# Two-layer latent transformer on one core: layer norms taken one token tile at a time, four landing places for the last head's values, and a reordered lead-in to the expert stage

## The chip, the core and the metric

The kernel runs on one core of a Trainium2 chip. The core has a matrix engine (PE, with its weight loads listed as PEld), a vector engine (DVE), an activation engine (ACT), GpSimd (POOL) and a queue engine (SP) that issues most transfers; sixteen DMA engines move the data. The five engines run their own instruction streams and meet at semaphores: one engine adds to a semaphore when an instruction is done, another waits for a value. The metric is the time of one execution in microseconds; lower is better.

## The reference

Six residual steps on a state `x` of 256 tokens by 512 features, each behind a layer norm without weights. The context has 4096 rows of 512.

```
x = x + cross_attention(norm(x), ctx)        # 16 heads of 128
x = x + attention_fp8(norm(x))               # 16 heads of 32, q, k, v rounded to e4m3 with one scale each
x = x + relu_ffn(norm(x)) + gate * expert    # 8 gate logits, 2 best
x = x + memory_attention(norm(x), ctx)       # scores against ctx, the 54 best of 4096 kept
x = x + attention(norm(x))                   # 16 heads of 32, with biases
x = x + moe(norm(x))                         # 64 experts, 8 per token, at most 64 tokens each
```

`norm(x)` is `(x - mean) / sqrt(var + 1e-5)` over the 512 features of a token.

## The kernel before

Everything is float32; where a product needs less time, an operand is split into a high and a low part of type fp32r and three products replace one. The 256 tokens are two tiles of 128 (`TT = 2`, `x[:, 0]` and `x[:, 1]`), the 512 features four blocks (`DT = 4`). The order of the work on each engine is written out by hand: one function for each engine and stage (`tensor_attention`, `vector_memory` and so on), called one after the other at the end of the program.

**The norm.** `vector_norm` takes the statistics of both tiles (L116, L119), adds the epsilon (L121), waits for GpSimd's power of -1/2 (L133) and writes the normed tiles `xn` (L126). `tensor_norm` fills PE's time with products of the identity (`stay_awake`, L138), then transposes the tiles (L146), and `scalar_norm` copies them to `xT` (L153), features on the partitions. Each stage's products wait for both tiles.

**Cross attention.** The 16 heads run one after the other; a head's 4096 keys are eight chunks of 512 (`NCH = 8`). The values of all heads are computed once and kept in DRAM (`v_dram`). For each chunk GpSimd loads them back (L867) into `v_back`, and from head 12 on (`LATE`) in turn into `v_back` and `v_late`. In the last head no keys are left to compute, so a chunk is only: DVE subtracts the maximum (`shift`, L694), ACT raises (L538) and rounds to `e_hi` (L547), DVE forms `e_lo` (L714), and PE multiplies by the values (`weigh`, L405, 12 products) and by ones for the sums (L410, 8 products). `load_v(n + 1)` waits until `weigh` has finished with the chunk that held its place. SP meanwhile loads the weights of the next stage (L950), one megabyte each for queries, keys and values, as `e_lo` of every second chunk is done.

**Attention, twice** (`k = 0` with quantisation, `k = 1` without). PE computes the eight feature blocks of queries and keys for both tiles (256 columns each), then the values of tile 0 and tile 1. For `k = 0` DVE needs the largest magnitude of all queries, GpSimd spreads it over the partitions, ACT and DVE round to e4m3, and then the same for the keys; only then do the scores start (L974).

**Feed-forward.** Products with `w_up`, then for each tile the gate, the expert and `w_down`.

**Memory attention.** Queries for both tiles, 16 blocks of scores (12 products each), a search for the 54 best on DVE, transposes of the weights (L1400), 16 blocks of products with the context (`weigh_chunk`, L1410), and for each tile a transpose (L1417) and the output product.

**Experts (MoE).** Router products and top 8 give `mask`, and ranks by products with triangular ones give `slot`, the place of a token in its expert. `make_sel` turns slots into 0/1 matrices `sel`; `gather` multiplies the tokens (`xn_hi`, `xn_lo`) by them. The slots also go transposed as `slotT` to DRAM and back as `slot_all`, spread over the partitions (L1663, L1666), for `make_selT` (L1839), which `spread_out` needs. The 64 experts are 32 pairs in groups of four; a turn of the loop is `up` (L1712), a `gather` of the next group, `down` (L1732, L1733), `spread_out` (L1741) and `turn` (L1723); once per group `find_gates` multiplies `sel` by the gate weights, 8 products. Weights of a pair come 2.3 MB at a time into a ring of seven.

A float32 product shows as two records in the trace, an fp32r product and a transpose as one.

## Time and profile before

| | |
|---|---|
| time of three runs | 1778.22, 1778.88, 1780.69 us, median 1778.88 |
| profiled execution | 1774.9 us, its span 1772.9 us |
| busy: PE / DVE / ACT / POOL | 1704.4 / 1088.1 / 693.3 / 96.4 us |
| granted PE clock over the span | 0.991 of full speed |
| instructions | 23791 |

The span runs from the first to the last instruction; around it the profiled execution has 2.0 us more. The busy time of PE includes the products of the identity, which compute nothing. A granted clock of 1 is 2.4 GHz; the other level is 1.2 GHz.

### The profile page before, as it was taken

Reading aid. Unit: us, or ns where it says so; the run is one execution under the profiler, and the core shown is the slowest. Engines: PE = TensorE matmul, PEld = TensorE weight load, DVE = VectorE, ACT = ScalarE, POOL = GpSimd, SP = SyncE. Lnnn points to the kernel's source line nnn. Section 1 sums busy time; section 2 is a strip of 40 time slices with the busy share of each in tenths; the row PEclk is TensorE's granted clock in tenths of the full one; section 3 lists DMA queues with packets and bytes.
Section 4 is the critical chain, followed back from the end, with each engine's and each line's share of the span. In section 5 each row is a group of like instructions: output and inputs, shape, how many; then the busy total and the mean of one; then the engine's idle time right before and its main releaser. Section 6 shows DMA issues by size and latency. Waiting matters only on the chain.

```text
span 1772.9 us, 23791 instructions
## 1 busy us (share of the span) xinstructions
PE 1704.4 (96%) x9438; PEld 1343.0 (76%) x9438; DVE 1088.1 (61%) x1738; ACT 693.3 (39%) x937; POOL 96.4 (5%) x177
## 2 busy tenths in 40 slices
PE   8998999999999999999999999978899999899998
PEld 7887888887888888788888788876577466554544
DVE  4446777777677777777777788965538315333333
ACT  4334444445444444444444555542213212212121
POOL 0000000000000000000000010010000000000000
PEclk9999999999999999999999999999999999999999
DMA  6755544445455454454454522252104181488880
GB/s 220 207 166 155 131 131 131 126 131 149 121 132 143 121 137 123 140 143 119 131 136 125 132 96 88 86 192 94 49 1 190 48 356 81 102 307 324 306 323 33
DMA packets 114733, 262.55 MB, mean 148 GB/s; under 512 B 6656, under 2 KB 76480, under 8 KB 108480
## 3 DMA queue, kind: packets, MB, share of 16 engines
q1 hardware_dynamic: 96192, 193.93, 35.5%
q0 software_dynamic: 18432, 67.12, 12.6%
q8 instruction: 75, 1.23, 0.3%
q14 instruction: 34, 0.28, 0.1%
HBM read 193.35 MB, written 67.67 MB: 147 GB/s over the span
## 4 chain that ended last, share of the span: by engine, by line
PE 64%; issue 24%; DVE 5%; DMA 3%; POOL 2%; ACT 1%; SPq 0%; POOLq 0%; DVEq 0%; ACTq 0%
PE bank L41 16%; PE bank L392 14%; PE bank L364 10%; PE bank L405 5%; PE bank L1712 5%; PE bank L1410 3%; PE bank L1733 2%; PE bank L1732 2%; PE bank L138 2%; PE bank L1741 2%; POOL v_back L867 1%; DMA v_dram<-v_out 1%; PE bank L1019 1%; DMA slot_all<-slots_dram 1%; PE bank L430 1%
## 5 line engine op out<-in xcount | busy, mean ns | idle before, releaser
L714 DVE TENSOR_TENSOR e_lo<-S,e_hi 128x1024 fp32r<-128x1024 f32 x128 | 156.6, 1223 | 94.1 <-ACT e_hi L547 93.8
L364 PE MATMUL bank<-cT_hi,wk_hi 128*128 128x512 f32 x512 | 205.6, 402 | 0.0
L392 PE MATMUL bank<-wv_hi,cT_hi 128*128 128x512 f32 x512 | 199.9, 390 | 3.5 <-DVE wv_lo L651 3.5
L364 PE MATMUL bank<-cT_hi,wk_lo 128*128 128x512 f32 x512 | 200.5, 392 | 0.0
L392 PE MATMUL bank<-wv_hi,cT_lo 128*128 128x512 f32 x512 | 199.4, 390 | 0.0
L364 PE MATMUL bank<-cT_lo,wk_hi 128*128 128x512 f32 x512 | 199.2, 389 | 0.0
L392 PE MATMUL bank<-wv_lo,cT_hi 128*128 128x512 f32 x512 | 199.2, 389 | 0.0
L538 ACT ACTIVATE S<-S 128x1024 f32<-128x1024 f32 x128 | 135.6, 1059 | 157.9 <-DVE S L694 157.8
L547 ACT CAST e_hi<-S 128x1024 fp32r<-128x1024 f32 x128 | 134.7, 1052 | 152.3 <-PE bank L405 142.7
L707 DVE TENSOR_TENSOR esum<-esum,S 128x512 f32<-128x512 f32 x210 | 145.1, 691 | 71.9 <-ACT S L538 68.3
L405 PE MATMUL bank<-e_hi,v_back 128*128 128x256 f32 x896 | 170.6, 288 | 12.2 <-DMA v_back<-v_dram 4.3
L682 DVE TENSOR_TENSOR mx<-mx,S 128x512 f32<-128x512 f32 x224 | 154.3, 689 | 15.1 <-ACT S L532 11.2
L41 PE MATMUL bank<-q_hi,k_hi 128*128 128x256 f32 x512 | 145.5, 284 | 15.6 <-ACT S L532 8.0
L694 DVE TENSOR_TENSOR S<-S,mrow 128x1024 f32<-128x1024 f32 x128 | 155.1, 1216 | 1.3 <-POOL mrow L873 1.3
L405 PEld LDWEIGHTS bank<-e_hi,v_back 128*128 128x128 f32 x896 | 141.8, 193 | 18.1 <-issue 11.6
L41 PE MATMUL bank<-q_lo,k_hi 128*128 128x256 f32 x512 | 145.6, 284 | 0.0
L41 PE MATMUL bank<-q_hi,k_lo 128*128 128x256 f32 x512 | 145.5, 284 | 0.0
L518 ACT CAST k_hi<-bank 128x512 fp32r<-128x512 f32 x128 | 75.1, 587 | 166.6 <-PE bank L364 166.6
L532 ACT COPY S<-bank 128x1024 f32<-128x1024 f32 x128 | 128.8, 1006 | 10.2 <-PE bank L41 10.2
L405 PE MATMUL bank<-e_lo,v_back 128*128 128x256 f32 x448 | 127.3, 284 | 0.0
L41 PEld LDWEIGHTS bank<-q_hi,k_hi 128*128 128x128 f32 x512 | 98.1, 192 | 23.9 <-DVE k_lo L669 10.1
L669 DVE TENSOR_TENSOR k_lo<-bank,k_hi 128x512 fp32r<-128x512 f32 x128 | 87.9, 687 | 45.3 <-ACT k_hi L518 45.3
(265 smaller groups left out, 2899.8 us busy)
## 6 DMA issues: line engine op xcount, KB each, us to landing
w<-in_w_moe SPq DMA_DIRECT2D x32, 2304.0 KB, 8.5
v_dram<-v_out SPq DMA_DIRECT2D x112, 512.0 KB, 4.6
v_back<-v_dram POOLq DMA_DIRECT2D x112, 512.0 KB, 5.0
v_dram<-v_back SPq DMA_DIRECT2D x16, 512.0 KB, 3.9
v_late<-v_dram POOLq DMA_DIRECT2D x16, 512.0 KB, 3.5
ctx_nat<-in_ctx SPq DMA_DIRECT2D x8, 1024.0 KB, 4.6
ctx_raw<-in_ctxT SPq DMA_DIRECT2D x7, 1024.0 KB, 8.0
l_w_qkv<-in_l_wqkv SPq DMA_DIRECT2D x6, 1024.0 KB, 6.0
```

Source lines behind the costliest of these rows:

```text
L41: last = e.matmul(dst, lhs, rhs, start=(n == 0), stop=(n == len(terms) - 1))
L364: t = e.matmul(banks[b][:], l, r, start=(c == 0 and m == 0), stop=(c == DT - 1 and m == 2))
L392: t = e.matmul(banks[b][:], l, r, start=(c == 0 and m == 0), stop=(c == DT - 1 and m == 2))
L405: t = e.matmul(banks[O_BANK][:, 0:T], v[:, i, l, :], r[:, i, :], start=(j == 0 and i == 0 and m == 0), stop=(j == NCH - 1 and i == CT - 1 ...
L532: e.copy(S[:, j * CT:(j + 1) * CT, :].rearrange("p a t -> p (a t)"), twin[:]).then_inc(s_stored, 1)
L538: e.activation(Sj, Sj, ACT.Exp).then_inc(raised, 1)
L547: e.copy(e_place(n)[0][:], S[:, j * CT:(j + 1) * CT, :]).then_inc(e_rounded, 1)
L682: own.done(e.tensor_tensor(mx[:], mx[:], two, ALU.max))
L694: e.tensor_tensor(Sj, Sj, mrow[:].unsqueeze(1).to_broadcast([P, CT, T]), ALU.subtract).then_inc(shifted, 1)
L707: e.tensor_tensor(esum[:], esum[:], two, ALU.add).then_inc(e_summed, 1)
L714: e.tensor_tensor(lo[:], Sj, hi[:].bitcast(F32), ALU.subtract).then_inc(e_split, 1)
L1712: t = e.matmul(banks[UP_BANKS[p % 2]][rows, 0:2 * FF], xg[:, g % 2, c, at:at + P // 2], ring[p % N_RING][:, s * UPW + c * 2 * FF:s * UPW + ...
```

## The change

**The norm by tiles.** `norm_stats`, `norm_apply`, `norm_turn` and `norm_move` each take one tile, and GpSimd raises one column at a time. Each stage is then laid out anew around them:

- in attention 0, tile 0's values are multiplied before tile 1 is transposed; queries and keys come behind that, for both tiles;
- in the feed-forward, gate and expert of tile 0 stand before tile 1's transpose, and tile 0's norm is taken while PE still projects tile 1's attention output;
- in memory attention, tile 0's queries stand before tile 1's transpose, and tile 1's queries between the second and the third block of scores; the seven small operations of `find_coefficient` stand between tile 1's statistics and its norm;
- in attention 1, the transpose of tile 0 and its queries, keys and values stand in the end of the memory stage, around tile 1's output product.

**Values in four places.** For the last head's eight chunks the values land in turn in `v_back`, `v_late`, `v_tail0` and `v_tail1`; the two new places lie on buffers that the last keys have left. The loads of chunks 1, 2 and 3 are issued together, each later one when the chunk four before it has been weighed.

**The lead-in to the experts.** The router and its logits go by tiles. `xn_hi` and `xn_lo` are formed early. The slots are transposed and moved out before the first `gather`, and `slot_all` comes in two parts, first the four pairs of the first group, then the other 28, for which only `make_selT(4)` waits. The gate weights are split into two fp32r parts, so that `find_gates` has 8 fp32r products of 4 columns for 8 float32 products of 2 columns.

```diff
+        def norm_stats(e, n, i):
+
+            own.done(e.bn_stats(stats[:, i, :], x[:, i, :]))
             own.wait(e)
-            for i in range(TT):
-                own.done(e.bn_aggr(meanvar[:, i, :], stats[:, i, :]))
+            own.done(e.bn_aggr(meanvar[:, i, :], stats[:, i, :]))
             own.wait(e)
-            e.tensor_scalar(vareps[:], meanvar[:, :, 1], EPS, None, ALU.add).then_inc(ln_var, 1)
...
+            e.tensor_scalar(vareps[:, i:i + 1], meanvar[:, i, 1:2], EPS, None, ALU.add).then_inc(ln_var, 1)
+
+        def norm_apply(e, n, i, xn):
+            e.wait_ge(ln_rstd, TT * n + i + 1)
+            e.tensor_scalar(xn[:, i, :], x[:, i, :], meanvar[:, i, 0:1], rstd[:, i:i + 1], ALU.subtract, ALU.mult).then_inc(ln_xn, 1)
...
-            e.wait_ge(ln_var, n + 1)
-            e.tensor_tensor(rstd[:], vareps[:], half[:], ALU.pow).then_inc(ln_rstd, 1)
+            for i in range(TT):
+                e.wait_ge(ln_var, TT * n + i + 1)
+                e.tensor_tensor(rstd[:, i:i + 1], vareps[:, i:i + 1], half[:, i:i + 1], ALU.pow).then_inc(ln_rstd, 1)
...
+        def norm_turn(e, n, i, xn, bank):
+
+            e.wait_ge(ln_xn, TT * n + i + 1)
+            for c in range(DT):
+                t = e.transpose(bank[:, c * P:(c + 1) * P], xn[:, i, c * P:(c + 1) * P], ident[:])
+            t.then_inc(ln_turned, 1)
...
+            b = late % 2 if n < TAIL else (n - TAIL) % 4
+            turns = late // 2 if n < TAIL else (TAIL - LATE * NCH) // 2 * (b < 2) + (n - TAIL) // 4
+            return (v_back, v_late, v_tail0, v_tail1)[b], v_in[b], 16 * (turns + 1 + (LATE * NCH if b == 0 else 0))
...
+            xn1 = att_mem[0][5]
+            for i in range(TT):
+                add_tile(h, i)
+                e.wait_ge(x_added, TT * h + i + 1)
+                norm_stats(e, 1, i)
+            for i in range(TT):
+                norm_apply(e, 1, i, xn1)
...
+                elif n - TAIL in (2, 3):
+                    e.wait_ge(scored, NH)
+                    e.wait_ge(k_projected, NH)
+                elif n > TAIL + 1:
+                    e.wait_ge(weighed, n - 3)
...
+                    elif n < TAIL:
                         load_v(n + 1)
+                    elif n == TAIL:
+                        for ahead in (1, 2, 3):
+                            load_v(n + ahead)
+                    elif n + 3 < NH:
+                        load_v(n + 3)
...
+        def project_qk(e, k, features, lo, hi):
+
+            w = att_mem[k][0]
+            for f in features:
+                if f % 4 == 0:
+                    e.wait_ge(att_w_in[f // 4], ATT_W[k])
+                t = matmuls(e, banks[f // 2][:, f % 2 * T + lo:f % 2 * T + hi],
+                            [(w[:, f // 4, c, f % 4 * P:(f % 4 + 1) * P], xT[:, c, lo:hi]) for c in range(DT)])
+                if f % 2 and hi == T:
+                    t.then_inc(qk_projected, 1)
+
+        def project_values(e, k, i):
+            w = att_mem[k][0]
+            e.wait_ge(att_w_in[2], ATT_W[k])
+            e.wait_ge(ln_xT, TT * (1 if k == 0 else 4) + i + 1)
+            matmuls(e, banks[4 + i][:], [(xT[:, c, i * P:(i + 1) * P], w[:, 2, c, :]) for c in range(DT)]).then_inc(av_projected, 1)
...
+            if k == 0:
+                stay_awake(e, banks[0], 12)
+                norm_turn(e, 1, 0, xn, banks[0])
+                stay_awake(e, banks[3], 2)
+                project_values(e, k, 0)
+                norm_turn(e, 1, 1, xn, banks[1])
+                e.wait_ge(ln_xT, TT * 2)
+                project_qk(e, k, range(8), 0, T)
+                project_values(e, k, 1)
+            else:
+                norm_turn(e, 4, 1, xn, av_bank(1))
+                stay_awake(e, av_bank(0), 2)
+                e.wait_ge(ln_xT, TT * 5)
+                project_qk(e, k, range(8), P, T)
+                project_values(e, k, 1)
...
             for i in range(TT):
+                own.done(e.tensor_tensor(x[:, i, :], x[:, i, :], b_out[:], ALU.add))
+            own.wait(e)
+            n_norm, xn_next = ((2, xn3), (5, xn6))[k]
+            for i in range(TT):
                 n = TT * k + i
...
                 e.tensor_tensor(x[:, i, :], banks[2 + i][:], x[:, i, :], ALU.add).then_inc(att_added, 1)
+                e.wait_ge(att_added, n + 1)
+                norm_stats(e, n_norm, i)
+                norm_apply(e, n_norm, i, xn_next)
...
+            norm_turn(e, 2, 0, xn3, banks[0])
+            stay_awake(e, banks[4], 2)
+            e.wait_ge(ln_xT, TT * 2 + 1)
+            gate(0)
+            expert(0)
+            norm_turn(e, 2, 1, xn3, banks[1])
+            stay_awake(e, banks[4], 2)
             e.wait_ge(ln_xT, TT * 3)
...
+            gate(1)
+            e.wait_ge(up_moved, DT // 2)
+            down(0)
+            expert(1)
+            down(1)
...
+            weights(0)
+            add_expert(0)
+            weights(1)
+            add_shared(0)
+            norm_apply(e, 3, 0, xn4)
+            add_expert(1)
+            add_shared(1)
+            find_coefficient(e)
+            norm_apply(e, 3, 1, xn4)
...
+                    if n == 2:
+                        project_q4(1)
+                    if n == NCH:
+                        e.wait_ge(q4_split, TT)
...
+            def project_q4(i):
+                tok = slice(i * P, (i + 1) * P)
+                e.wait_ge(*landed["w_q4"])
+                e.wait_ge(ln_xT, TT * 3 + i + 1)
+                for f in range(DT):
+                    t = matmuls(e, q4_bank(f)[:, tok], [(w_q4[:, c, f * P:(f + 1) * P], xT[:, c, tok]) for c in range(DT)])
+                t.then_inc(q4_projected, 1)
+
+            norm_turn(e, 3, 0, xn4, banks[0])
+            stay_awake(e, twin, 2)
+            project_q4(0)
+            norm_turn(e, 3, 1, xn4, banks[1])
+            stay_awake(e, banks[score4_bank(0)], 4)
+            e.wait_ge(q4_split, 1)
             score_tile(0)
             score_tile(1)
             for s in range(TT * NCH + 1):
                 if s < TT * NCH:
                     turn(*divmod(s, NCH))
+                if s == TT * NCH:
+                    norm_turn(e, 4, 0, att_mem[1][5], av_bank(0))
                 if s:
                     weigh_chunk(*divmod(s - 1, NCH))
                 if s == NCH + 2:
                     turn_av(0)
                 if s == NCH + 4:
                     project_out(0)
+            e.wait_ge(ln_xT, TT * 4 + 1)
+            e.wait_ge(p_moved, TT * NCH)
+            project_qk(e, 1, range(4), 0, P)
             turn_av(1)
+            project_qk(e, 1, range(4, 8), 0, P)
             project_out(1)
+            project_values(e, 1, 0)
...
-                e.dma_start(slot_all[rows], by_half[s].unsqueeze(0).to_broadcast([P // 2, PAIRS, T])).then_inc(slots_in, 16)
+                e.dma_start(slot_all[rows, 0:FIRST], by_half[s, 0:FIRST].unsqueeze(0).to_broadcast([P // 2, FIRST, T])).then_inc(slots_in, 16)
+            e.wait_ge(slots_in, 32)
+            for s, rows in enumerate(halves):
+                e.dma_start(slot_all[rows, FIRST:], by_half[s, FIRST:].unsqueeze(0).to_broadcast([P // 2, PAIRS - FIRST, T])).then_inc(slots_in, 16)
...
-                    two = slice(EPP * (GROUP * g + n), EPP * (GROUP * g + n + 1))
-                    t = matmuls(e, TURN_B[:, 2 * P + 2 * n:2 * P + 2 * n + 2],
-                                [(sel[:, g % 2, i, pair].bitcast(F32), gate_w[:, i, two]) for i in range(TT)])
+                    t = matmuls(e, TURN_B[:, 2 * P + 4 * n:2 * P + 4 * n + 4],
+                                [(sel[:, g % 2, i, pair], gate_parts[:, i, GROUP * g + n, :, :]) for i in range(TT)])
...
             for i in range(TT):
-                matmuls(e, banks[2][:, i * E:(i + 1) * E],
+                stay_awake(e, banks[i], 2 + 8 * i)
+                norm_turn(e, 5, i, xn6, banks[i])
+                stay_awake(e, banks[4], 2)
+                e.wait_ge(ln_xT, TT * 5 + i + 1)
+                matmuls(e, banks[2 + i][:, 0:E],
                         [(xT[:, c, i * P:(i + 1) * P], w_router[:, c, :]) for c in range(DT)]).then_inc(routed, 1)
...
-            for c in range(DT):
-                gather(0, c)
             e.wait_ge(slot_made, 1)
             for i in range(TT):
                 t = e.transpose(TURN_B[0:E, i * P:(i + 1) * P], slot[:, i, :], ident[:])
             t.then_inc(slot_turned, 1)
+            for c in range(DT):
+                gather(0, c)
...
             for i in range(TT):
+                e.wait_ge(logits_moved, i + 1)
                 own.done(e.max(route(i, 8, 16), logit[:, i, :]))
+                if i == 0:
+                    e.wait_ge(xn_rounded, 1)
+                    e.tensor_tensor(xn_lo[:], xn6[:], xn_hi[:].bitcast(F32), ALU.subtract).then_inc(xn_split, 1)
...
-            e.wait_ge(xn_rounded, 1)
-            e.tensor_tensor(xn_lo[:], xn6[:], xn_hi[:].bitcast(F32), ALU.subtract).then_inc(xn_split, 1)
+            e.wait_ge(slot_turned, 1)
+            e.tensor_copy(slotT[:], TURN_B[0:E, 0:T]).then_inc(slot_moved, 1)
...
+                high, low_part = gate_parts[:, i, :, 0, :], gate_parts[:, i, :, 1, :]
+                gates = gate_w[:, i, :].rearrange("p (n s) -> p n s", s=EPP)
+                own.done(e.tensor_scalar(high, gates, route(i, 2), None, ALU.mult))
+                own.wait(e)
+                e.scalar_tensor_tensor(low_part, gates, route(i, 2), high.bitcast(F32), ALU.mult, ALU.subtract).then_inc(route_gate, 1)
```

The core of the diff is shown; left out are declarations, renamings and the same steps on ACT.

**Three places in the order of instructions.** The first is GpSimd's stream at the last head: `v_...<-v_dram` is one load of a chunk's values (L867, in the new kernel L887), `mrow<-mxr` the maximum of the last head over the partitions, for which the head's first `shift` waits. Before:

```order
L867 DMA v_late<-v_dram 128x1024
L873 ISA mrow<-mxr 128x256
L867 DMA v_back<-v_dram 128x1024
L867 DMA v_late<-v_dram 128x1024
L867 DMA v_back<-v_dram 128x1024
L867 DMA v_late<-v_dram 128x1024
```

Now:

```order
L887 DMA v_late<-v_dram 128x1024
L887 DMA v_tail0<-v_dram 128x1024
L887 DMA v_tail1<-v_dram 128x1024
L893 ISA mrow<-mxr 128x256
L887 DMA v_back<-v_dram 128x1024
L887 DMA v_late<-v_dram 128x1024
L887 DMA v_tail0<-v_dram 128x1024
L887 DMA v_tail1<-v_dram 128x1024
```

Two loads moved ahead of the maximum, and four are left behind it instead of six.

The second is PE's stream between the last head and the first scores of attention 0 (`l0_xn` is the normed state, `l0_w_qkv` the weights; 256 wide are queries and keys of both tiles, 512 wide the values of one tile). Before:

```order
L138 MATMUL bank0<-ident 128x128 x20
L146 MATMUL bank0<-ident,l0_xn 128x128 x4
L146 MATMUL bank1<-ident,l0_xn 128x128 x4
L138 MATMUL bank3<-ident 128x128 x2
L41 MATMUL bank0<-xT,l0_w_qkv 128x256 x8
L41 MATMUL bank1<-xT,l0_w_qkv 128x256 x8
L41 MATMUL bank2<-xT,l0_w_qkv 128x256 x8
L41 MATMUL bank3<-xT,l0_w_qkv 128x256 x8
L41 MATMUL bank4<-l0_w_qkv,xT 128x512 x4
L41 MATMUL bank5<-l0_w_qkv,xT 128x512 x4
```

Now:

```order
L135 MATMUL bank0<-ident 128x128 x12
L141 MATMUL bank0<-ident,l0_xn 128x128 x4
L135 MATMUL bank3<-ident 128x128 x2
L41 MATMUL bank4<-l0_w_qkv,xT 128x512 x4
L141 MATMUL bank1<-ident,l0_xn 128x128 x4
L41 MATMUL bank0<-xT,l0_w_qkv 128x256 x8
L41 MATMUL bank1<-xT,l0_w_qkv 128x256 x8
L41 MATMUL bank2<-xT,l0_w_qkv 128x256 x8
L41 MATMUL bank3<-xT,l0_w_qkv 128x256 x8
L41 MATMUL bank5<-l0_w_qkv,xT 128x512 x4
```

The values of tile 0 and tile 1's transpose moved ahead of all queries and keys.

The third is PE's stream from the last block of products with the context (`ctx_nat`) to the values of attention 1 (`av` is the memory attention's result, `w_o4` its output weights). Before:

```order
L1410 MATMUL bank5<-ctx_nat,pT 128x512 x8
L1417 MATMUL bank67<-ident,av 128x128 x4
L41 MATMUL bank3<-w_o4,xT 128x512 x4
L138 MATMUL bank0<-ident 128x128 x14
L146 MATMUL bank0<-ident,l1_xn 128x128 x4
L146 MATMUL bank1<-ident,l1_xn 128x128 x4
L138 MATMUL bank3<-ident 128x128 x2
L41 MATMUL bank0<-xT,l1_w_qkv 128x256 x8
```

Now:

```order
L141 MATMUL bank67<-ident,l1_xn 128x128 x4
L1495 MATMUL bank5<-ctx_nat,pT 128x512 x4
L41 MATMUL bank0<-xT,l1_w_qkv 128x128 x8
L41 MATMUL bank1<-xT,l1_w_qkv 128x128 x8
L1502 MATMUL bank67<-ident,av 128x128 x4
L41 MATMUL bank2<-xT,l1_w_qkv 128x128 x8
L41 MATMUL bank3<-xT,l1_w_qkv 128x128 x8
L41 MATMUL bank5<-w_o4,xT 128x512 x4
L41 MATMUL bank4<-l1_w_qkv,xT 128x512 x4
L141 MATMUL bank67<-ident,l1_xn 128x128 x4
L135 MATMUL bank67<-ident 128x128 x2
L41 MATMUL bank0<-xT,l1_w_qkv 128x128 x8
```

The 14 products of the identity are gone, and tile 0's queries, keys and values stand on both sides of tile 1's output product.

## Rows read from the trace of the kernel before

**Rows 1.** Three stretches: us, busy of PE, PEld, DVE, ACT, POOL, granted clock, DMA share, GB/s
```profile
1180.60:1184.50 3.90, 3.82 (x20) 3.69 (x20) 1.43 (x2) 0.00 (x0) 0.00 (x0) 0.62 0.93 342
...
1529.70:1534.10 4.40, 4.40 (x18) 1.59 (x18) 1.61 (x4) 0.00 (x0) 0.00 (x0) 0.62 0.78 142
...
1545.20:1740.00 194.80, 194.80 (x943) 98.12 (x943) 63.83 (x182) 38.97 (x78) 0.00 (x0) 1.00 0.79 300
```
**Rows 2.** Timeline of PE, last head: start, us, instruction [idle before <- releaser]
```profile
1172.99 0.48 PE L405 MATMUL bank<-e_hi,v_late 128*128 128x256 f32 x2 [1.16 <-DVE e_lo L714]
...
1175.90 0.50 PE L405 MATMUL bank<-e_hi,v_back 128*128 128x256 f32 x2 [0.28 <-DMA v_back<-v_dram]
...
1180.68 0.50 PE L405 MATMUL bank<-e_hi,v_late 128*128 128x256 f32 x2 [2.13 <-DMA v_late<-v_dram]
...
1193.90 0.50 PE L405 MATMUL bank<-e_hi,v_back 128*128 128x256 f32 x2 [2.70 <-DMA v_back<-v_dram]
...
1200.16 0.28 PE L410 MATMUL bank<-e_lo,ones_r 128*128 128x256 f32 x1
```
**Rows 3.** Timeline of ACT and DVE, last head, chunk 4
```profile
1178.59 1.04 ACT L547 CAST e_hi<-S 128x1024 fp32r<-128x1024 f32 x1 [0.92 <-PE bank L410]
...
1179.66 1.22 DVE L714 TENSOR_TENSOR e_lo<-S,e_hi 128x1024 fp32r<-128x1024 f32 x1 [0.56 <-ACT e_hi L547]
```
**Rows 4.** Timeline of POOL before the last head
```profile
1161.52 0.53 POOL L867 DMA_DIRECT2D v_late<-v_dram  x1 [2.32 <-PE bank L405]
1163.11 1.06 POOL L873 PARTITION_ALL_REDUCE mrow<-mxr  x1 [1.07 <-DVE mxr L687]
```
**Rows 5.** Timelines of DVE and PE, norm and products of attention 0
```profile
1207.81 1.39 DVE L126 TENSOR_SCALAR l_xn<-x,meanvar,rstd 128x512 f32<-128x512 f32 x2 [0.87 <-POOL rstd L133]
1218.45 1.22 DVE L1138 TENSOR_REDUCE l_sc<-l_qkT 128x1 f32<-128x1024 f32 x1 [9.25 <-ACT l_qkT L1085]
...
1208.80 1.11 PE L146 MATMUL bank<-ident,l_xn 128*128 128x128 f32 x8 [0.73 <-DVE l_xn L126]
...
1210.62 14.08 PE L41 MATMUL bank<-xT,l_w_qkv 128*128 128x256 f32 x64 [0.26 <-ACT xT L153]
1224.54 7.03 PE L41 MATMUL bank<-l_w_qkv,xT 128*128 128x512 f32 x16
```
**Rows 6.** Timeline of PE, from attention 0's output product to the feed-forward
```profile
1277.14 3.29 PE L138 MATMUL bank<-ident 128*128 128x128 f32 x28
...
1283.13 7.17 PE L41 MATMUL bank<-xT,w_up 128*128 128x256 f32 x32 [0.25 <-ACT xT L153]
```
**Rows 7.** Timeline of PE, from the feed-forward to the memory scores
```profile
1305.66 3.29 PE L138 MATMUL bank<-ident 128*128 128x128 f32 x28
...
1320.17 0.50 PE L41 MATMUL bank<-cT_hi,qT_hi 128*128 128x512 f32 x1 [0.29 <-DVE qT_lo L1582]
```
**Rows 8.** Timeline of PE, from the memory stage to attention 1's scores
```profile
1423.42 7.03 PE L1410 MATMUL bank<-ctx_nat,pT 128*128 128x512 f32 x16
...
1442.34 14.08 PE L41 MATMUL bank<-xT,l_w_qkv 128*128 128x256 f32 x64 [0.26 <-ACT xT L153]
...
1463.22 1.14 PE L974 MATMUL bank<-l_qkT 32*128 32x256 f32 x12
```
**Rows 9.** Timelines of DVE and PE, start of the expert stage
```profile
1521.78 1.22 DVE L1889 TENSOR_TENSOR xn_lo<-xn,xn_hi 128x1024 fp32r<-128x1024 f32 x1
...
1527.32 0.42 DVE L1899 CAST slotT<-bank 64x256 bf16<-64x256 f32 x1 [3.06 <-PE bank L1761]
...
1543.60 0.35 DVE L1839 TENSOR_SCALAR selT<-slot_all,slot_col 128x256 fp32r<-128x256 bf16 x1 [7.10 <-DMA slot_all<-slots_dram]
...
1527.88 1.92 PE L41 MATMUL bank<-gate_w,sel 128*128 128x2 f32 x16 [0.60 <-DVE slotT L1899]
1529.73 4.43 PE L1712 MATMUL bank<-w,xg 128*64 128x384 f32 x16
...
1544.78 0.44 PE L1723 MATMUL bank<-ident,h 128*128 128x128 f32 x2 [2.81 <-DVE h L1855]
```

232 lines of the change are left out of this document (104 added, 128 removed).

## The prediction

> **What bounds the kernel now.** I read the chain of waits first: it runs through PE's products almost everywhere, with DVE, ACT and DMA links only in the seams between stages. The stretches by window confirm it: in the expert loop PE is busy all 194.8 us at full granted clock [rows 1], so there only fewer PE records help. Then I read each engine's timeline around every norm and at the end of cross attention, for what PE waits for there. The reader should see three things. In the last head PE waits for values from DRAM, up to 2.70 us before a chunk [rows 2], and then runs some products at a lower clock, 0.62 on average in one stretch [rows 1]. At each norm PE fills 3.29 us with identity products and then still waits, because nothing starts until both tiles are normed, turned and copied [rows 5 to 8]. At the start of the expert stage a transfer, `slot_all`, holds DVE for 7.10 us and through it PE for 2.81 us [rows 9].
>
> **The last head.** Chunk 1 starts at 1172.99 and chunk 2 could have started at 1175.90 - 0.28 = 1175.62, so a chunk takes 2.63 us when its values are there [rows 2]. Does another engine hold a chunk longer? `e_hi` of chunk 4 starts when chunk 2 has left its buffer, and ACT's 1.04 and DVE's 1.22 us after it end at 1180.88 [rows 3], 2.3 us after that start; chunk 3 is weighed meanwhile, which is the longer. So seven chunks follow 1172.99 at 2.63: end at 1191.4, against 1200.44 now [rows 2]: **-9.0**. The four loads now go out some three chunks (7.9 us) before their use instead of one. But the four loads (0.5 MB each) and three blocks of attention weights (1 MB each) must move 5.2 MB before the last chunk starts at 1188.8, from about 1172.4: 320 GB/s, where 342 is what the busy stretch moved [rows 1]. At 270 GB/s the last load would be some 3 to 4 us late; so the gain lies between 5 and 9.3. I take 9.0, since the weights of the values are asked for only near the end. On POOL two more loads stand before the maximum: three loads of 0.53 from 1161.52 end at 1163.11, exactly where the reduction starts now [rows 4]. I cost that at nothing; the cover is DVE's own maximum, and should it be gone, DVE's first `shift`, and every chunk behind it, is late by at most 0.5.
>
> **Attention 0.** DVE takes both statistics before the first norm; tile 0 then needs no wait for GpSimd (0.87 idle in [rows 5]), less two more handovers: 0.65 earlier. Turning and copying both tiles took 1210.62 - 1208.80 = 1.82; one tile I estimate at 1.3, one copy of about half a microsecond less. Tile 0's values take half of 7.03, 3.5 [rows 5]. Behind them tile 1 is turned and copied, 1.3 in which PE has nothing. Queries start later by -0.65 + 1.3 + 3.5 + 1.3 - 1.82 = **+3.6**. Is that hidden? No: DVE waits 9.25 us for exactly these queries before it can look for their magnitude [rows 5], and the rounding of the keys, and the scores, come one after the other behind it. The values, which are computed earlier, were never waited for. This is the part of the change that I expect to cost. Its bounds: 2.6 if keys had some slack behind queries, 5.6 if PE's clock falls, since 8 of the 20 identity products are gone and PE stands for some 2 us before tile 0 comes.
>
> **Feed-forward.** Tile 0 is normed while PE projects tile 1's output. From 1277.14 to 1283.13 PE had 5.99 us without useful work [rows 6]; now it has two turnings of 1.3 and 0.1 of wait, with gate and expert of tile 0 between them, long enough (4.4) for tile 1's norm: **-3.3** (bounds 2 and 3.5).
>
> **Memory.** From 1305.66 to 1320.17 are 14.51 us [rows 7], which hold two halves of 3.6 for the queries. Now: turn tile 0 (1.3), its queries (3.6), then rounding and splitting them beside tile 1's transpose (1.5): 6.4, and tile 1's queries later among the scores (3.6). 14.5 - 10.0 = **-4.4** with 0.1 for handovers (bounds 3 and 4.6). `find_coefficient`, seven small operations, stands in GpSimd's time and PE's, which is with tile 0's queries then; without that cover it costs 1.4.
>
> **Attention 1.** From 1430.45 (1423.42 + 7.03) to 1463.22 are 32.8 us [rows 8], with 24.6 of products (14.08, 7.03 and an output product of 3.5). Now the stalls are tile 0's transpose and that of `av`, 0.4 each, and one turning of 1.3 behind tile 0's values, which cover tile 1's norm (3.5 against some 3.5); 0.4 more for handovers. 32.8 - 27.1 = **-5.7** (bounds 4 and 6). Products over 128 columns instead of 256 are twice as many at half the length; the identity products, 3.29 for 28 records [rows 6], show 0.118 a record at that width, where 14.08 for 64 [rows 5] is 0.22 at twice the width, so splitting by tiles adds only 0.3 us here, which I count.
>
> **Start of the expert stage.** `up(0)` starts at 1529.73 [rows 9]. Off the path go `xn_lo` (1.2), the wait for `slotT` (0.6), half of the gate products' 1.92 (0.9), and 0.5 from logits by tiles, where the ten identity products before tile 1's transpose eat most of the norm's gain: -3.2. `up(0)` took 4.43 at a clock of 0.62 [rows 1]; at full clock that is 2.75. The fall came after short products with few columns, of which fewer are left, so -1.6. Then PE's wait of 2.81 behind `slot_all` [rows 9]. `slotT` is out at about 1522.2 instead of 1527.74. The whole table was there 15.9 us after it; the first part is an eighth. It is needed at about 1531.5; even half of 15.9 would do. Sum **-7.6** (bounds 4.5 and 8).
>
> **Gates in the loop.** Each group spends 16 records on 8 products; a record takes 0.12 at 2 columns [rows 9], the same as 128 columns, so the record counts, not the columns. Eight fp32r records for 16: 0.9 less, in seven groups on a PE that is always busy: **-6.3**. No fp32r product this narrow is in the trace: the bounds are 0 (it takes what two float32 records take) and 6.5. I take 6.3, since a chunk of 20 fp32r products in the last head takes 2.63 us [rows 2], 0.13 each at 256 columns.
>
> Norm 0 I cost at nothing: identity products outlast it. The sum is -9.0 + 3.6 - 3.3 - 4.4 - 5.7 - 7.6 - 6.3 = -32.7. The profiled execution, 1774.9 us, would become 1742.2. The median of the runs is 4.0 above it, so 1746.2; I say 1746.
>
> **The rivals.**
> *Values still late.* The loads share the engines with the attention weights and only 5 of the 9 us come. For it: DMA was saturated in [rows 1]. Against: 7.9 us lead instead of one chunk's. Time 1750. Chance 0.12.
> *Narrow fp32r products are no cheaper.* Nothing from the gates, here or at the start: 7.2 lost, 1753. Against it the record of 0.12 at either width. Chance 0.10.
> *The clock falls in the new seams.* Some 28 identity records stood in each of four seams; real products replace part of them, and transposes and waits the rest. What it costs is in [rows 1]: 4.4 us at 0.62 instead of 1, 1.6 us each time; in five seams 8 us: 1754. For it: stalls of 2 us in [rows 2] were followed by such a stretch. Against: the new stalls are about 1.3 us. Chance 0.14. The Trainium skill, "TensorE: Matmul & The Clock Gate", Part 4: PE-mode transpose, says that a transpose does not count as activity for the clock as other products do; by it the seams, now built of transposes and waits, would fall to the lower level, and it speaks for this rival. No stretch of this trace has transposes alone.
> *Attention 0 pays nothing.* Its delay is hidden behind something that I took for serial: 1743. Against: DVE's 9.25 us of wait. Chance 0.06.
> *Handovers by tile are dearer than counted*, by half of each seam's gain (10 us): 1756. Chance 0.06.
> *Slower.* The expert loop's PE loses its clock, since eight records per group go. At 0.62, work takes 1.6 times as long, so 54 us of the 195 at that level eat the 32.7 and decide; 80 us at it cost 48: 1794. Against: 1.00 over the whole stretch, and other products keep PE busy. Chance 0.02.
>
> **The numbers.** The forecast as worked out, within some 4 us, has 0.46, and what I have not named 0.04, mostly near no change. A measurement of this kernel tells 0.2%, 3.6 us, from no change. All but the last rival and the unnamed lie below 1775: faster 0.94, within 0.2% 0.03, slower 0.03. The range reaches from attention 0 paying nothing with the best bounds, 1740, to the clock rival with a further loss, 1758.
>
> **What would show it.** Right: the last head's chunks 2.6 us apart with no DMA named before them, and a second granted clock near 1; attention 0's queries starting 5 to 6 us after its first transpose; `up(1)` not followed by a wait for `slot_all`; eight gate records per group in under 1 us. The prediction is wrong if loads with more than 3 us of PE's idle time remain in the last head, if gate products still take 1.8 us a group, if the granted clock in any seam is under 0.8, or if DVE starts on attention 0's queries no later than before.

## The result and the profile after

| | before | changed |
|---|---|---|
| runs | 1778.07 to 1780.69 us (4) | 1745.16 to 1748.93 us (4) |
| median | 1778.55 us | 1746.42 us |
| ratio | | 0.9819, 95% interval 0.9802 to 0.9836 |
| profiled execution, its span | 1774.9, 1772.9 us | 1748.93, 1747.2 us |
| instructions | 23791 | 23699 |

The prediction was 1746 us. The medians differ by 32.1 us and the profiled pair by 26.0: before's profiled execution was shorter than all its runs above, and the changed kernel's was its longest. The reading goes seam by seam, a seam being the place where one stage hands over to the next. First the changed kernel's last head, timelines of POOL and PE (start, us, instruction, [idle before <- releaser]), beside [rows 2, 4]:

```profile
1161.77 0.53 POOL L887 DMA_DIRECT2D v_late<-v_dram  x1 [2.32 <-PE bank L403]
1162.86 1.05 POOL L887 DMA_DIRECT2D v_tail<-v_dram  x2 [0.56 <-issue]
1163.93 1.03 POOL L893 PARTITION_ALL_REDUCE mrow<-mxr  x1
...
1181.83 0.53 POOL L887 DMA_DIRECT2D v_tail<-v_dram  x1 [2.20 <-PE bank L408]
...
1170.00 0.47 PE L403 MATMUL bank<-e_hi,v_back 128*128 128x256 f32 x2 [1.61 <-DVE small L734]
1173.78 0.47 PE L403 MATMUL bank<-e_hi,v_late 128*128 128x256 f32 x2 [1.16 <-DVE e_lo L716]
1190.12 0.51 PE L403 MATMUL bank<-e_hi,v_tail 128*128 128x256 f32 x2 [1.07 <-DMA v_tail<-v_dram]
1193.24 1.98 PE L428 MATMUL bank<-wqo_raw,oT 128*128 128x512 f32 x4 [0.46 <-ACT oT L561]
```

One wait of 1.07 us for values is left of four, and the output product starts at 1193.24 (before: 1200.90). The maximum starts 2.16 us after the `v_late` load instead of 1.59 [rows 4]: the two loads in front of it are not free. They don't follow the first load at once, either: POOL stands idle for 0.56 us between them.

Attention 0, timeline of PE, beside [rows 5]:

```profile
1200.27 0.66 PE L141 MATMUL bank<-ident,l_xn 128*128 128x128 f32 x4 [1.64 <-DVE l_xn L123]
1200.76 0.61 PE L135 MATMUL bank<-ident 128*128 128x128 f32 x4
1201.69 5.37 PE L41 MATMUL bank<-l_w_qkv,xT 128*128 128x512 f32 x8 [0.32 <-ACT xT L146]
1206.89 0.60 PE L141 MATMUL bank<-ident,l_xn 128*128 128x128 f32 x4
1208.17 14.08 PE L41 MATMUL bank<-xT,l_w_qkv 128*128 128x256 f32 x64 [0.68 <-ACT xT L146]
1222.09 3.60 PE L41 MATMUL bank<-l_w_qkv,xT 128*128 128x512 f32 x8
1230.37 0.61 PE L1016 MATMUL bank<-l_k,l_q 32*128 32x256 bf16 x6 [4.68 <-DVE l_k L1206]
1230.91 2.08 PE L135 MATMUL bank<-ident 128*128 128x128 f32 x8
```

The queries and keys take 14.08 us as before. Behind them only 3.60 us of values are left where 7.03 stood, while ACT and DVE take as long as ever to quantise queries and keys; so PE stands still for 4.68 us (before: 1.26). The identity products after it take 2.08 us for 8 records; before they took 1.16. Windows of the same trace (us, busy of PE, PEld, DVE, ACT and POOL with their instructions, granted clock, DMA share, GB/s):

```profile
1201.70:1207.00 5.30, 5.30 (x9) 2.21 (x10) 0.00 (x0) 0.00 (x0) 0.11 (x1) 0.68 0.01 3
...
1230.00:1242.00 12.00, 10.29 (x68) 7.36 (x68) 8.92 (x24) 2.79 (x4) 0.35 (x1) 0.59 0.41 168
1242.00:1257.00 15.00, 12.35 (x120) 9.68 (x124) 9.57 (x15) 5.25 (x10) 0.00 (x0) 0.77 0.00 1
1257.00:1274.00 17.00, 13.52 (x164) 9.47 (x156) 7.73 (x11) 5.21 (x9) 0.00 (x0) 0.90 0.01 1
...
1274.40:1454.00 179.60, 178.14 (x762) 117.31 (x762) 77.44 (x254) 39.61 (x66) 4.61 (x9) 1.00 0.37 144
1492.00:1525.40 33.40, 32.41 (x177) 21.38 (x178) 15.80 (x48) 8.71 (x16) 3.06 (x11) 1.00 0.30 52
```

Of the stages that the change laid out anew, attention 0 alone has the low clock. The feed-forward, the memory stage and the first products of attention 1 (179.6 us, PE idle for 1.5) and the lead-in to the experts run at 1.00. The start of the expert stage, timelines of DVE and PE, beside [rows 9]:

```profile
1510.45 0.42 DVE L2011 CAST slotT<-bank 64x256 bf16<-64x256 f32 x1 [0.22 <-PE bank L1875]
1520.09 0.35 DVE L1960 TENSOR_SCALAR selT<-slot_all,slot_col 128x256 fp32r<-128x256 bf16 x1
...
1514.04 0.95 PE L41 MATMUL bank<-gate_parts,sel 128*128 128x4 f32 x8
1514.92 2.80 PE L1826 MATMUL bank<-w,xg 128*64 128x384 f32 x16
1519.16 0.44 PE L1837 MATMUL bank<-ident,h 128*128 128x128 f32 x2 [0.31 <-DVE h L1976]
1525.36 0.38 PE L1837 MATMUL bank<-ident,h 128*128 128x128 f32 x2
```

No wait is named before `selT`, the gate products take 0.95 us in place of 1.92, `up(0)` 2.80 in place of 4.43, and the second transpose of the hidden values no longer waits.

Here is the span cut at seven points, for the profiled pair and for a second pair of profiles of the same two kernels (labels b0 and a0 below). The points are: the start of weighing chunk 0 of the last head (L403, before L405), the reciprocal of the head's sums (DVE), attention 0's first query product, its first scores, its first output product, that of attention 1, the end.

| stretch (us) | before | changed | before, 2nd | changed, 2nd |
|---|---|---|---|---|
| start to chunk 0 | 1169.21 | 1170.00 | 1169.88 | 1172.06 |
| to the reciprocal (last head) | 34.24 | 25.79 | 31.28 | 25.92 |
| to the first query | 7.17 | 12.38 | 7.17 | 10.69 |
| to the first scores | 22.21 | 22.20 | 22.21 | 22.20 |
| to output product 0 | 37.34 | 44.02 | 40.23 | 44.03 |
| to output product 1 | 232.67 | 217.60 | 231.06 | 217.60 |
| to the end (experts) | 270.06 | 255.21 | 271.47 | 255.20 |

The low clock is not new in attention 0. In both profiles of the kernel before, and in all nine later ones that have this wait of 2.24 us, the clock falls behind it (timeline of PE of the kernel before; 12 identity products take 1.60 us at full clock):

```profile
1249.99 0.61 PE L974 MATMUL bank<-l_k,l_q 32*128 32x256 bf16 x6 [2.24 <-DVE l_mx L1166]
1250.53 2.86 PE L138 MATMUL bank<-ident 128*128 128x128 f32 x12
```

### The profile page after: what moved, and what is told of

Read it like the earlier page. It is cut to its first block, busy times and chain, and to the rows that moved or that the text cites. A ratio compares the mean times of both kernels' runs of the same rounds, so it can differ in the third digit from the quotient of the medians.

```text
span 1747.2 us, 23699 instructions
## 1 busy us (share of the span) xinstructions
PE 1688.3 (97%) x9372; PEld 1328.4 (76%) x9372; DVE 1090.4 (62%) x1746; ACT 694.0 (40%) x938; POOL 99.0 (6%) x183
## 3 DMA queue, kind: packets, MB, share of 16 engines
q0 software_dynamic: 18432, 67.12, 13.4%
## 4 chain that ended last, share of the span: by engine, by line
PE 75%; issue 13%; DVE 5%; DMA 3%; ACT 2%; POOL 1%; SPq 0%; DVEq 0%; POOLq 0%; ACTq 0%
PE bank L41 18%; PE bank L390 17%; PE bank L362 13%; PE bank L403 7%; PE bank L1826 5%; PE bank L1495 3%; PE bank L135 2%; PE bank L1847 2%; PE bank L1846 2%; DMA v_dram<-v_out 2%; PE bank L1855 2%; PE bank L1061 1%; PE bank L428 1%; DVE l_inv L1231 1%; DMA v_out<-in_wv 1%
## 5 line engine op out<-in xcount | busy, mean ns | idle before, releaser
L403 PE MATMUL bank<-e_hi,v_back 128*128 128x256 f32 x880 | 167.7, 288 | 8.7 <-DVE small L734 4.6
L403 PEld LDWEIGHTS bank<-e_hi,v_back 128*128 128x128 f32 x880 | 139.1, 192 | 14.8 <-issue 8.1
L403 PE MATMUL bank<-e_lo,v_back 128*128 128x256 f32 x440 | 124.9, 284 | 0.0
```

The source lines that it names most:

```text
L403: t = e.matmul(banks[O_BANK][:, 0:T], v[:, i, l, :], r[:, i, :], start=(j == 0 and i == 0 and m == 0), stop=(j == NCH - 1 and i == CT - 1 ...
```

## The experiments

Each kernel is the changed one with the edit named, unless said otherwise. Differences are those of medians against 1746.44 us, the changed kernel's in a0. a0 and e1 to e3 were measured together, e4 to e7 together, and e8 last; the kernel before had medians of 1779.24, 1778.54 and 1779.76 us beside them, so a difference of about 1 us between these groups says nothing. The head groups are the stretch from attention 0's first scores to its first output product.

**The changed kernel and the kernel before, once more (no edit).**

> The changed kernel once more, beside the others of its call. Theory A (in attention 0 TensorE waits 4.68 us for the quantised keys with nothing to do, because half of the value products that used to fill this wait now stand ahead of the queries; its clock then stands at the low level through the first head groups): 1745 to 1749 us again, and the same low clock between the first scores and the output product, 76 to 79 us from the reciprocal of the last head's sums to the first output product. Theory B (the low clock there was chance in one execution; the profiled run was the slowest of four): this stretch is 70 us or less and the clock is near full.

Measured: 1746.44 us (5 runs, 1742.91 to 1750.08), ratio 0.9812 [0.9796, 0.9828]. Its profile shows the same 4.68 us wait and 44.03 us of head groups, and 76.9 us from the reciprocal to the output product, so theory B falls as far as these two profiles go. But the 1.7 us that tile 0's values lost in the first profile (5.37 against 3.67) are not there: that part was chance. In the profiles of later variants with the same code in attention 0 the head groups take 43.99, 42.04, 39.04, 42.09 and 39.09 us: how much low clock follows the wait differs between executions. From the reciprocal on that is 71.9 to 76.9 us, so theory A's 76 to 79 don't hold for all of them.

> The kernel before once more, for a second profile. Question: the changed kernel is 26 us shorter in the profiled pair, but 32 us by the medians. Theory A: the profiled execution of the kernel before was one of its shortest because its clock stayed up in attention 0 (37.3 us from the first scores to the output product) and this one shows 39 to 42 us there, with all stretches outside the two attentions and the last head within 0.2 us. Theory B: the difference sits elsewhere, in transfers or in the head loop before the last head.

Measured: one run, 1775.31 us. Both theories are partly right. The head groups took 40.23 us (granted clock 0.87, against 0.95 in the first profile), which is theory A. But the last head took 31.28 in place of 34.24, and that was nearly all the clock and hardly the waits for transfers: its four waits for values sum to 6.12 us (first profile: 6.43), while PE's granted clock in the head was 1.00 here and 0.90 there, with 2.7 us less of busy time. And 1.4 us more went to the clock right behind PE's 2.76 us wait at the start of the experts (0.97 over 56.3 us, where the first profile has 1.00). Windows around the last head in the kernel before, first and second profile:

```profile
1164.00:1202.00 38.00, 28.86 (x200) 26.85 (x199) 20.37 (x19) 17.00 (x18) 3.36 (x7) 0.91 0.60 202
...
1164.00:1202.00 38.00, 29.10 (x214) 25.87 (x213) 21.09 (x21) 16.99 (x18) 4.04 (x7) 1.00 0.63 212
```

The total came out nearly the same, and why other runs of this kernel are up to 6 us longer no profile here shows.

**Attention 0 in its old order (e1).**

```diff
                 norm_turn(e, 1, 0, xn, banks[0])
-                stay_awake(e, banks[3], 2)
-                project_values(e, k, 0)
                 norm_turn(e, 1, 1, xn, banks[1])
+                stay_awake(e, banks[3], 2)
                 e.wait_ge(ln_xT, TT * 2)
                 project_qk(e, k, range(8), 0, T)
+                project_values(e, k, 0)
                 project_values(e, k, 1)
```

> Attention 0 in its old order: both tiles turned, then queries and keys, then both tiles' values; all else as changed. Theory A: the 3.5 us that the values of tile 0 add ahead of the queries go, with the 1.8 us that they lost to the clock and the 6.7 us that the head groups took longer; 66 to 67 us from the reciprocal to the output product in place of 78.6, so 10 to 12 us less than the changed kernel in a profile, and 1735 to 1738 us. Theory B: only what the prediction's term says comes back, 3.6 us, and 1742 to 1743 us.

Measured: 1740.01 us (1738.04 to 1744.11), ratio 0.9785 [0.9771, 0.9798]: 6.4 us less. The first query starts 6.97 us after the reciprocal, which is 3.7 sooner than in seven of the eight profiles with the new order, and the wait for the keys is back at 1.26. That is between the theories: B's 3.6 is seen in the profile, and 2.8 us are left for the clock, not 8. These 2.8 are about what the 95% intervals reach to either side (2.4 and 2.8 us), and the profile doesn't show where they come from. It has 71.34 us from the reciprocal to the output product, where theory A expected 66 to 67 and the seven profiles with the new order and its wait have 71.9 to 78.6. PE's clock fell at other waits instead: the queries and keys, behind waits of 1.64 and 0.51 us, took 15.50 us and not 14.08, and the head groups 40.75 (timeline of PE):

```profile
1224.21 0.40 PE L1016 MATMUL bank<-l_k,l_q 32*128 32x256 bf16 x6 [1.26 <-DVE l_k L1206]
...
1232.95 1.80 PE L135 MATMUL bank<-ident 128*128 128x128 f32 x12 [1.15 <-ACT l_eT L1149]
...
1234.77 3.37 PE L135 MATMUL bank<-ident 128*128 128x128 f32 x16
```

The 16 records of the last row take 2.00 us at full clock.

**The new order with its two waits filled (e2).**

```diff
-                stay_awake(e, banks[0], 12)
+                stay_awake(e, banks[0], 19)
                 norm_turn(e, 1, 0, xn, banks[0])
...
                 project_values(e, k, 1)
+                stay_awake(e, W_BANK, 18)
```

> The new order is kept, but the two waits of TensorE in attention 0 are filled with dummy products: 7 more (14 records) ahead of tile 0's transposes, which came after 1.64 us of waiting, and 18 (36 records, 4.2 us) in the 4.68 us wait ahead of the first scores. Theory A: the order costs its 3.5 us still, but the clock stays high, so the 1.8 and most of the 6.7 us come back: 7 to 8.5 us less than the changed kernel, 1738 to 1740 us. Theory B: fillers in waits give nothing, 1745 to 1749 us.

Measured: 1742.93 us (1738.77 to 1746.97), ratio 0.9795 [0.9778, 0.9812]: 3.5 us less. The order's 3.5 us stays (first query 10.69 after the reciprocal) and the scores start at full clock, and the head groups take 38.99 us. Against a0's 44.03 that looks like theory A, but e5 and e7, which have the long wait unfilled, took 39.04 and 39.09; so one profile doesn't show what the filling is worth. In the times it gives half of what I expected. The clock fell again at two later waits (1.16 and 2.24 us) that I had not filled, and that may be why.

**Two landing places (e3).** `v_ring` and `load_v` as before the change.

```diff
-            b = late % 2 if n < TAIL else (n - TAIL) % 4
+            b = late % 2
...
-                    elif n < TAIL:
-                        load_v(n + 1)
-                    elif n == TAIL:
-                        for ahead in (1, 2, 3):
-                            load_v(n + ahead)
-                    elif n + 3 < NH:
-                        load_v(n + 3)
+                    elif n + 1 < NH:
+                        load_v(n + 1)
```

> The values of the last head come back in two places again, each load behind the weighing before it; all else as changed. Theory A (the change bought 7.7 us here in the profiled pair, of the 9.0 in the prediction): 7.5 to 8 us more than the changed kernel, 1754 us. Theory B: the term of 9.0 us is right and the 1.3 us were lost elsewhere: 1755 to 1756 us. Theory C: the two extra loads merely moved the wait to the attention weights that share the queues, 2 us or less: 1748 us.

Measured: 1755.03 us (1749.98 to 1756.74), ratio 0.9855 [0.984, 0.9871]: 8.6 us more. The waits are back (timeline of PE):

```profile
1183.33 0.80 PE L403 MATMUL bank<-e_hi,v_late 128*128 128x256 f32 x2 [3.06 <-DMA v_late<-v_dram]
1191.90 0.50 PE L403 MATMUL bank<-e_hi,v_late 128*128 128x256 f32 x2 [0.98 <-DMA v_late<-v_dram]
1197.08 0.50 PE L403 MATMUL bank<-e_hi,v_back 128*128 128x256 f32 x2 [2.53 <-DMA v_back<-v_dram]
```

From chunk 0 to the reciprocal it takes 34.48 us; with four places it took 24.77 to 25.92 in nine profiles. Theory C falls. A and B are 1.3 us apart, too close for the times; the profiles, 8.6 to 9.7 us apart, side with the term of the prediction. Not all of it is waiting. The waits for values here sum to 6.95 us, and the granted clock over the stretch is 0.90, where the profiles with four places have 1.00.

**The two extra loads behind the maximum (e7).**

```diff
                     elif n == TAIL:
-                        for ahead in (1, 2, 3):
-                            load_v(n + ahead)
+                        load_v(n + 1)
...
                         largest_score(h)
+                    if n == TAIL:
+                        load_v(n + 2)
+                        load_v(n + 3)
```

> GpSimd issues the two extra value loads of the last head behind its all-reduce in place of ahead of it; all else as changed. Theory A (the two issues, 0.5 us each, hold the all-reduce and with it the last head's first exponentials and weighing): the last head begins 0.6 to 0.8 us sooner after its scores, 1745.7 us; the third and fourth loads are issued 1 us later and still land before they are wanted. Theory B (covered): no difference. Either is less than the interval of the times; the profile's instants tell them apart.

Measured: 1743.79 us (1742.46 to 1746.23), ratio 0.9803 [0.9789, 0.9816]. Timeline of POOL:

```profile
1163.11 0.53 POOL L887 DMA_DIRECT2D v_late<-v_dram  x1 [2.32 <-PE bank L403]
1164.71 1.06 POOL L893 PARTITION_ALL_REDUCE mrow<-mxr  x1 [1.06 <-DVE mxr L689]
1165.64 1.08 POOL L887 DMA_DIRECT2D v_tail<-v_dram  x2
```

The maximum follows the load by 1.60 us, as before the change, and chunk 0 by 7.70 (before: 7.69). In the seven profiles with the two loads in front, chunk 0 follows by 8.11 to 8.39. Theory A, with 0.4 to 0.7 us; the rest of the 2.7 us in the median is within what the runs scatter.

**Gates with float32 products (e4).**

```diff
-                    t = matmuls(e, TURN_B[:, 2 * P + 4 * n:2 * P + 4 * n + 4],
-                                [(sel[:, g % 2, i, pair], gate_parts[:, i, GROUP * g + n, :, :]) for i in range(TT)])
+                    two = slice(EPP * (GROUP * g + n), EPP * (GROUP * g + n + 1))
+                    t = matmuls(e, TURN_B[:, 2 * P + 2 * n:2 * P + 2 * n + 2],
+                                [(sel[:, g % 2, i, pair].bitcast(F32), gate_w[:, i, two]) for i in range(TT)])
```

> The gates of a slot are found with float32 products two columns wide again, in place of fp32r ones four wide; all else as changed. Theory A (by count of passes: half the records, 0.9 us a group of four pairs, eight groups, one of them in the lead-in): 6.5 to 7.5 us more than the changed kernel, 1753 to 1754 us, and 16 records of 1.84 us a group. Theory B (the group is not on the path, another wait takes its place in each group): 2 us more or less, 1746 to 1748 us.

DVE's splitting of the gate weights and its adding of the two parts go back too, which the cut leaves out.

Measured: 1754.72 us (1752.46 to 1758.2), ratio 0.9869 [0.9854, 0.9884]: 8.3 us more. In the profile the lead-in grows by 0.89 us and the loop by 6.28, which is theory A to a tenth. Groups of PE's products in the loop (line, operation, names, shapes, count | busy us, mean ns), this kernel first and the changed one in the second fence:

```profile
L41 PE MATMUL bank<-gate_w,sel 128*128 128x2 f32 x112 | 12.9, 246 | 0.0
```

```profile
L41 PE MATMUL bank<-gate_parts,sel 128*128 128x4 f32 x56 | 6.6, 240 | 0.0
```

This run shows one thing more. The 16 narrow records stand ahead of `up(0)` again, and it still takes 2.80 us (timeline of PE):

```profile
1510.18 1.84 PE L41 MATMUL bank<-gate_w,sel 128*128 128x2 f32 x16
1511.95 2.80 PE L1827 MATMUL bank<-w,xg 128*64 128x384 f32 x16
```

**Slot numbers whole (e5).**

```diff
-                e.dma_start(slot_all[rows, 0:FIRST], by_half[s, 0:FIRST].unsqueeze(0).to_broadcast([P // 2, FIRST, T])).then_inc(slots_in, 16)
-            e.wait_ge(slots_in, 32)
-            for s, rows in enumerate(halves):
-                e.dma_start(slot_all[rows, FIRST:], by_half[s, FIRST:].unsqueeze(0).to_broadcast([P // 2, PAIRS - FIRST, T])).then_inc(slots_in, 16)
+                e.dma_start(slot_all[rows], by_half[s].unsqueeze(0).to_broadcast([P // 2, PAIRS, T])).then_inc(slots_in, 16)
```

> The slot numbers are spread over the partitions whole, 16 pairs and more a half, in place of four pairs first and the rest behind; all else as changed. Theory A: the second turn of the hidden values or the first spreading waits some 2.8 to 3.2 us for them, as before the change: 1749 to 1750 us. Theory B (the earlier issue alone hides them, since the numbers now leave sooner beside the products): 1746 us, no difference.

Measured: 1749.44 us (1746.43 to 1753.85), ratio 0.9841 [0.9828, 0.9854]: 3.0 us more, theory A; 2.6 of it stand in the profile up to the second transpose of the hidden values. DVE waits, and PE behind it:

```profile
1521.58 0.35 DVE L1955 TENSOR_SCALAR selT<-slot_all,slot_col 128x256 fp32r<-128x256 bf16 x1 [6.68 <-DMA slot_all<-slots_dram]
...
1522.75 0.44 PE L1834 MATMUL bank<-ident,h 128*128 128x128 f32 x2 [2.40 <-DVE h L1971]
```

**First gather ahead of the slots' transpose (e6).**

```diff
             stay_awake(e, GATHER_B, 7)
+            for c in range(DT):
+                gather(0, c)
             e.wait_ge(slot_made, 1)
...
             t.then_inc(slot_turned, 1)
-            for c in range(DT):
-                gather(0, c)
             find_gates(0)
```

> In the expert lead-in the gather of the first tokens (16 products, 3.8 us) stands ahead of the turning of the slot numbers again; all else as changed. Theory A (the slot numbers' way over DRAM is the longer chain, so turning them 3.8 us sooner is what keeps it hidden, while TensorE itself does the same work in either order): 2 to 4 us more, 1748 to 1750 us, with a wait for the slot numbers at the first spreading. Theory B (TensorE's own work sets the end of the lead-in): within 1 us of the changed kernel.

Measured: 1750.86 us (1747.02 to 1753.34), ratio 0.9839 [0.9826, 0.9852]: 4.4 us more, and 6.07 in the profile between output product 1 and the second transpose of the hidden values. The size is a little above theory A's, but its reason is wrong: no wait for `slot_all` is named anywhere. Timelines of DVE and PE:

```profile
1510.30 0.42 DVE L2011 CAST slotT<-bank 64x256 bf16<-64x256 f32 x1 [4.23 <-PE bank L1877]
...
1512.68 1.86 PE L41 MATMUL bank<-gate_parts,sel 128*128 128x4 f32 x8 [2.41 <-DVE gate_parts L2023]
1514.47 5.15 PE L1826 MATMUL bank<-w,xg 128*64 128x384 f32 x16
```

DVE waits 4.23 us for the transpose with the gates' own operations queued behind that copy; PE then waits 2.41 us for the gates, its clock falls, and `up(0)` takes 5.15 instead of 2.80. So what the order buys is that DVE works on the gates while PE gathers.

**All that helps (e8).** e1 and e7 together, more identity products in attention 0's waits, and eight of them moved in front of a wait.

```diff
-                stay_awake(e, banks[0], 12)
+                stay_awake(e, banks[0], 19)
...
+                stay_awake(e, W_BANK, 5)
...
+                    if f > 1 and k == 0:
+                        e.wait_ge(as_max, base + SHG * f - 1)
+                        stay_awake(e, banks[2], 9)
                     e.wait_ge(as_max, base + SHG * f)
...
+                if f == 1 and k == 0:
+                    stay_awake(e, W_BANK, 5)
...
+                short = f == 3 and k == 0
+                if short:
+                    stay_awake(e, banks[2], 8)
                 if f:
                     e.wait_ge(ao_moved, 4 * k + f)
                 if f in (0, 3):
-                    stay_awake(e, W_BANK, 8)
+                    stay_awake(e, W_BANK, 2 if short else 8)
```

> All that the runs so far speak for: attention 0 in its old order, GpSimd's two extra loads behind its all-reduce, and dummy products in the waits of attention 0 that have none (7 before tile 0's transposes, 5 before the first scores, 5 before the second group's turned maxima, 9 before the scores of the third and fourth groups once three of the four maxima of the bank's group are there), while 8 that overran the fourth group's exponentials by 1.4 us stand ahead of a wait instead. Theory A (what differs between executions in attention 0 is the clock after waits with nothing to do): full clock all through, 35.5 to 36.5 us from the first scores to the output product, where the runs so far had 37.3 to 44.0, 22.2 us from the first query product to the scores, 0.45 us less ahead of the last head, and 1732 to 1735 us. Theory B (the clock falls by where it stands in time and not by these waits): 39 to 44 us for that stretch, 1738 to 1742 us.

Measured: 1734.62 us (1733.43 to 1736.11), ratio 0.9751 [0.9736, 0.9767]: 11.8 us less than the changed kernel, and theory A. Two windows of its trace, the head groups and the stretch from first query to first scores:

```profile
1222.70:1258.80 36.10, 33.40 (x394) 25.56 (x394) 25.98 (x49) 13.26 (x22) 0.35 (x1) 1.00 0.22 87
1200.50:1222.70 22.20, 22.06 (x90) 16.39 (x90) 9.91 (x17) 7.88 (x10) 0.73 (x2) 1.00 0.03 5
```

The head groups take 36.07 us at a clock of 1.00; two waits of 0.8 us are the longest left in them. Its five runs lie within 2.7 us of each other, with a granted clock of 0.995 or 0.996 over the span, where those of the changed kernel spread over 7.2 with 0.988 to 0.992; so most of that spread seems to be the clock in this stage. It is faster than both kernels. How much of the 36.07 is owed to the eight products moved in front of a wait (an estimate from e1's instants is 1.4 us, since they outlast the exponentials by that) was not run by itself.

## Why the prediction was right

The time came out within 0.5 us of the forecast, and each term was measured within 1 us of its size, the last head's in all comparisons but one. Against the table and the experiments:

- **The last head, -9.0 and 0 for POOL.** Right in size. The stretch is 5.4 to 8.5 us shorter in the two pairs, 8.6 to 9.7 against e3's profile, and undoing it costs 8.6 in the times. In the pairs, the waits for values sink from 6.4 and 6.1 us to 1.1 and 1.2; another 2.7 us of the first pair are the low clock behind those waits, which only that profile and e3's have. "At nothing" for the two extra loads was wrong by 0.4 to 0.7 us. The working laid three loads of 0.53 end to end and so reached the old start of the maximum; in the trace an idle stretch of 0.42 to 0.72 us stands between the first and the other two. In some profiles a late chunk still waited for its values, up to 1.22 us. That its load, issued at 1181.83 in the first profile, meets the attention weights is my reading and was not tested. The rival "values still late" stayed that small.
- **Attention 0, +3.6.** The order costs 3.5 us (10.69 less 7.17). The term stopped too early, though. I followed the queries' delay and did not ask what PE would do in the time that the moved values had filled: 4.68 us of nothing behind the keys, and then products at a granted clock of 0.59. What that is worth is not settled. The seven profiles with the long wait have 39.04 to 44.03 us of head groups, mean 42.0; the three with the old order of products (before, twice, and e1) have 37.34, 40.23 and 40.75, mean 39.4. The means are 2.6 apart, and e1's median gives 2.8 beyond the order, but the ranges overlap.
- **Feed-forward, memory and attention 1, -3.3, -4.4 and -5.7.** From output product 0 to attention 1's first scores the profile has 179.59 us for 193.05: 13.46 less, forecast 13.4. One by one they are -3.2, -4.0 and -6.2; the transpose of tile 0, 0.4 us, changed sides between the last two. The working says that it counts 0.3 us for splitting attention 1's queries and keys by tiles, but its 27.1 doesn't hold them; by its own 0.118 a record the split would be 1.0 us, and it measured 0.5 (14.40 us for 128 records, 13.92 for 64 of twice the width).
- **Start of the experts, -7.6.** 33.37 us for 41.94: 8.6 less. The way to `up(0)` shrank by 4.0 and not 3.2, and the rest as said: 1.6 of clock and 2.8 of wait. The reason given for the clock was wrong. It was said to fall behind short products with few columns, but with all 16 of them back (e4) `up(0)` takes 2.80 us; in e6 it fell behind a wait of 2.41 us, and in the kernel before waits of 1.32 and 0.60 us stood ahead. That these waits were the cause there was not run by itself. e5 shows 2.6 of it in the profile for the two-part transfer and e4 0.9 for the gates. e6 shows that the early transpose of the slots works through DVE's queue, which the term did not name.
- **Gates in the loop, -6.3.** 6.28 in the profiles, in both directions (e4). The rival "narrow fp32r products are no cheaper" is refuted: 240 ns a record for fp32r and 246 for float32, and half the records.
- **The clock rival** (1754) was right about attention 0 alone. The Trainium skill, "TensorE: Matmul & The Clock Gate", Part 4: PE-mode transpose, says that a transpose doesn't count as busy in the same way for the clock. By it the new seams would be slow. The three seams that are made of groups of four transposes, a few identity products and real products ran at a granted clock of 1.00 over 179.6 us. A stretch of transposes alone is in none of these traces. None of the other rivals came true: attention 0's delay was not hidden, the handovers cost what was counted, and the loop ran at 1.00.
- **The signs.** One sign of being wrong came true: the granted clock in attention 0 was under 0.8, with 0.59 behind the first scores and 0.68 ahead of the first query. One sign of being right did not: the queries start 6.2 us after the first transpose in seven profiles and 7.9 in the first, not 5 to 6; the working's own terms add to 6.1. The others held, but for one late chunk.

The half microsecond is luck. The terms as measured give 33.5 us (8.6 + 13.5 + 8.6 + 6.3 less 3.5) and not 32.7; attention 0's clock, which the sum left out, takes some of it back, and the medians are 32.1 us apart. The runs of a single kernel lie up to 8 us apart, and the changed kernel's profiled execution, forecast at 1742.2, took 1748.93.

## What to carry to other kernels

When work is moved forward out of a queue, ask two things: what it now stands in front of, and which wait it used to fill. Here half of a 7 us block went from a place where PE worked on it while a quantising chain ran to a place where it delayed that chain. The delay cost 3.5 us; the empty place left a wait with the low clock behind it, whose price differs from one execution to the next. With identity products in all waits of the head groups over 0.8 us, and eight that outlasted one moved in front of another, the stage was at its fastest and the runs closest together (e8); the steps were not run one by one. Medians and one pair of profiles can disagree by 6 us of 30 when the clock differs between executions, so a term is best read from a stretch that repeats. The feed-forward and the memory stage do, to 0.1 us, in all profiles with the same code there, and so does the expert stage in the changed kernel; in the two profiles of the kernel before it differs by 1.4 us.
